# First layer: the experts' network moved from a stage of its own into the rounds of the attention

## The reference, cut to what matters

```python
xn = _layernorm(x)
# s: attention, 16 heads of 8 channels
attn = softmax(q @ k.T / sqrt(8)) * head_mask      # per head, 512 x 512 scores
s = (attn @ v) @ Wo.T + bo
# g: a shared network and eight experts of which two count per token
shared_out = swiglu(xn @ w_shared_in) @ w_shared_out
probs = softmax(xn @ w_gate + gate_bias);  top 2 of 8 kept, the rest set to 0
hid = swiglu(xn @ w1_shared)                       # the same for all experts
routed_out = sum_e probs_e * (hid @ w2[e])
x = x + s * silu(shared_out + routed_out)
```

## Time and profile before

| | us |
|---|---|
| three executions | 4061.76, 4041.41, 4063.99 (median 4061.76) |
| the profiled execution: own time | 4054.44 |
| the profiled execution: span | 4053.1 |
| busy in the span | PE 3121.8, DVE 2586.1, ACT 2027.6, POOL 1555.6 |
| mean granted clock of PE | 0.836 |

### The profile page before, as it was taken

How to read it: one execution, slowest core, us unless ns; L and a number is a source line. 1 busy time by engine, 2 the same in 40 slices (tenths; PEclk the granted TensorE clock), 3 DMA queues, 4 the chain that set the end, 5 groups by cost and what they waited for, 6 DMA issues and landing times.

```text
span 4053.1 us, 40791 instructions
## 1 busy us (share of the span) xinstructions
PE 3121.8 (77%) x14850; PEld 1366.2 (34%) x14850; DVE 2586.1 (64%) x2891; ACT 2027.6 (50%) x3628; POOL 1555.6 (38%) x938
## 2 busy tenths in 40 slices
PE   5777877975567777777875879766687888888886
PEld 2111212341222222222322643322144554555544
DVE  4676672438998788888877234487726655555553
ACT  1454453124456766666565221567444555555654
POOL 2211100113457666666757002244414444444432
PEclk6788897986678878877777879888698998999998
DMA  3111200011111121121111001000000000000000
GB/s 86 38 36 26 43 7 2 0 55 48 35 35 36 31 56 35 35 51 40 33 24 44 10 0 64 21 21 21 21 0 19 19 19 10 19 19 10 19 10 31
DMA packets 79733, 114.60 MB, mean 28 GB/s; under 512 B 16270, under 2 KB 49422, under 8 KB 78106
## 3 DMA queue, kind: packets, MB, share of 16 engines
q1 hardware_dynamic: 68268, 103.33, 10.5%
q0 software_dynamic: 11264, 8.66, 1.6%
HBM read 37.96 MB, written 17.33 MB: 14 GB/s over the span
## 4 chain that ended last, share of the span: by engine, by line
PE 50%; DVE 21%; ACT 16%; issue 6%; POOL 3%; DMA 2%; SPq 1%; POOLq 0%; DVEq 0%; ACTq 0%
DVE layer_mamba_state L1335 7%; DVE psum L1323 4%; PE psum L1107 3%; PE psum L774 3%; PE psum L2455 3%; PE psum L1184 3%; ACT layer_mamba_decay L1261 3%; PE psum L2486 3%; ACT layer_exps L787 2%; PE psum L238 2%; PE psum L2149 2%; PE psum L226 2%; PE psum L900 2%; PE psum L232 2%; PE psum L822 2%
## 5 line engine op out<-in xcount | busy, mean ns | idle before, releaser
L1364 POOL TENSOR_TENSOR layer_mamba_state<-layer_mamba_state,layer_mamba_c 128x1024 f32<-128x1024 f32 x320 | 780.4, 2448 | 597.1 <-DVE layer_mamba_state L1335 588.6
L1335 DVE TENSOR_TENSOR_SCAN layer_mamba_state<-layer_mamba_decay,psum 128x1024 f32<-128x1024 f32 x320 | 731.5, 2286 | 43.7 <-ACT layer_mamba_decay L1261 11.5
L1184 PE MATMUL psum<-layer_mamba_state,two_to_one 128*64 128x512 f32 x1280 | 443.7, 785 | 121.1 <-DVE layer_mamba_x L1352 77.0
L1261 ACT ACTIVATE layer_mamba_decay<-layer_mamba_delta_wide,layer_weights 128x511 f32<-128x511 f32 x640 | 415.6, 711 | 74.5 <-DMA layer_mamba_delta_wide<-layer_mamba_delta 38.2
L1323 DVE TENSOR_TENSOR psum<-psum,layer_mamba_u_wide 128x1024 f32<-128x1024 f32 x320 | 393.4, 1229 | 62.9 <-PE psum L1142 26.2
L714 DVE TENSOR_REDUCE layer_peak<-psum 128x2 f32<-128x1024 f32 x256 | 308.7, 1222 | 123.0 <-PE psum L685 118.4
L787 ACT ACTIVATE layer_exps<-psum 128x1024 f32<-128x1024 f32 x256 | 249.8, 1030 | 223.2 <-PE psum L754 223.2
L2852 POOL TENSOR_TENSOR layer_p<-layer_p,layer_stats 128x512 f32<-128x512 f32 x128 | 133.0, 1040 | 294.5 <-DVE layer_stats L2775 294.4
L2646 ACT ACTIVATE layer_p<-psum,layer_stats 128x128 f32<-128x128 f32 x512 | 181.2, 369 | 127.9 <-DVE layer_stats L2768 126.3
L1142 PE MATMUL psum<-layer_mamba_bc,layer_mamba_pick 96*64 96x512 bf16 x768 | 165.1, 457 | 91.2 <-DVE psum L1323 67.5
L2839 POOL TENSOR_TENSOR layer_qk<-layer_qk,layer_v_between 128x1024 f32<-128x1024 f32 x64 | 150.4, 2350 | 217.7 <-DVE layer_v_between L2739 215.9
(11 more groups left out here) (349 smaller groups left out, 6257.2 us busy)
## 6 DMA issues: line engine op xcount, KB each, us to landing
layer_mamba_delta_wide<-layer_mamba_delta SPq DMA_DIRECT2D x160, 128.0 KB, 2.3
layer_mamba_u_wide<-layer_mamba_work SPq DMA_DIRECT2D x160, 128.0 KB, 2.4
layer_v_between<-layer_v SPq DMA_DIRECT2D x16, 512.0 KB, 4.3
qk_dram<-layer_qk_parts SPq DMA_DIRECT2D x16, 384.0 KB, 2.6
layer_q_rows<-qk_dram SPq DMA_DIRECT2D x96, 64.0 KB
layer_k_rows<-qk_dram SPq DMA_DIRECT2D x96, 64.0 KB
layer_v_between<-layer_v SPq DMA_DIRECT2D x16, 384.0 KB, 5.6
layer_weights<-weights_dram SPq DMA_DIRECT2D x1, 4147.0 KB, 12.3
```

Source lines behind the costliest of these rows:

```text
L1184: e = pe.matmul(c.psum[j * HALF:(j + 1) * HALF, self.sum_banks[h], :], c.two_to_one[:, :], self.state[i % len(self.state)][:, j, :], start ...
L1261: e = act.activation(decay[:, j, 1:SEQ], self.delta_wide[h][:, j, 1:SEQ], ACT.Exp, scale=rates[:, rate:rate + 1])
L1335: dve.tensor_tensor_scan(state, decay, self.fill.rearrange("p j t -> p (j t)"), 0.0, ALU.mult, ALU.add).then_inc(self.scanned, 1)
L1364: pool.tensor_tensor(state, state, self.both(self.c_wide[turn % self.C_BUFFERS][:, :]), ALU.mult).then_inc(self.multiplied, 1)
```

## The change

`Ffn0` is no stage of its own any more. Its object is given to `Attention0`, whose `run` weaves the expert generators in with the others:

- **The choice of experts.** `Route` yields between its operations. Its first 8 steps are woven with project(0), after it in each round; the rest goes ahead of maxima(0) and project(1) in each round. The 64 logit records stand in its first step, so on PE they come behind the query product of sequence 0 and ahead of its key product. The transposes, eight rounds of four, all use bank 6.
- **The network.** `ffn(b)` is the last generator of iteration b, one sequence at a time, on bank 7 alone, and is silent for the first 7 rounds. On PE the four products of xn stand in rounds 7, 10, 12 and 15, the spreading of experts 0 to 3 in rounds 17 to 20, the shared output product and the experts' products in rounds 21 (three products) and 22 (two), experts 4 to 7 likewise in rounds 24 to 27, 28 and 29 (two each). ACT has SiLU in rounds 8 and 13, a Copy of the first half's total in round 22 and the gate's SiLU in round 30; DVE has the two swiglu products in rounds 10 and 15, the eight scalings in rounds 17 to 20 and 24 to 27, and the sum of the halves in round 29 or 30.
- **The update of x.** POOL multiplies and adds for sequence b-1 in round 7 of iteration b; for the last one after the last divide.
- Buffers are shared: the scaled inputs lie where the attention keeps its normed heads, and the choice works where it keeps its heads. The layer ends with one meeting of the engines less.

The arithmetic is the same but for the order of the sum over experts, now two halves of four. The other user of `Route`, in the third layer, plays its steps to the end at once, in the old order.

```diff
@@ Attention0.__init__ and run
-        weave(self.run(self.pe_project, self.pe_maxima, self.pe_attend, self.pe_divide))
-        weave(self.run(self.act_project, self.act_maxima, self.act_attend, self.act_divide))
-        weave(self.run(self.dve_project, self.dve_maxima, self.dve_attend, self.dve_divide))
-        weave(self.run(self.pool_project, self.pool_maxima, self.nothing, self.nothing))
+        weave(self.run(self.pe_project, self.pe_maxima, self.pe_attend, self.pe_divide, ffn.pe, self.nothing, route.pe()))
+        weave(self.run(self.act_project, self.act_maxima, self.act_attend, self.act_divide, ffn.act, self.nothing, route.act()))
+        weave(self.run(self.dve_project, self.dve_maxima, self.dve_attend, self.dve_divide, ffn.dve, self.nothing, route.dve()))
+        weave(self.run(self.pool_project, self.pool_maxima, self.nothing, self.nothing, self.nothing, ffn.pool, blank(0)))
...
-        weave(on(project, 0))
-        weave(on(maxima, 0), on(project, 1))
+        weave(on(project, 0), islice(route, self.CHOICE_BEFORE))
+        weave(route, on(maxima, 0), on(project, 1))
         for b in range(SEQS + 1):
-            weave(on(divide, b - 1), on(attend, b), on(maxima, b + 1), on(project, b + 2))
+            weave(on(divide, b - 1), on(attend, b), on(maxima, b + 1), on(project, b + 2), on(ffn, b), on(update, b - 1))
@@ Ffn0
+    BANK, BEHIND, PART = 7, 7, EXPERTS // 2
...
+    def pe(self, b):
+        c, pe, hold, w, rhs, bank = self.c, self.c.pe, self.c.pe_hold, self.w, self.xn[:, b, :], self.c.psum[:, self.BANK, :]
+        yield from blank(self.BEHIND)
+        hold.wait_ge(self.loaded, 16)
         for i, name in enumerate(("w_shared_in", "w1_shared")):
+            c.wait_bank(self.BANK)
+            pe.matmul(bank, w[name][:, 0:P], rhs, start=True, stop=True).then_inc(self.halves_made, 1)
+            c.bank_read[self.BANK] = self.silu_made, 2 * b + i + 1
             yield from blank(3)
+            c.wait_bank(self.BANK)
+            pe.matmul(bank, w[name][:, P:2 * P], rhs, start=True, stop=True).then_inc(self.halves_made, 1)
+            c.bank_read[self.BANK] = self.glu_made, 2 * b + i + 1
+            yield from blank(2)
+        for part in range(2):
+            experts = range(part * self.PART, (part + 1) * self.PART)
+            for n in experts:
                 hold.wait_ge(self.route.rows_made, b + 1)
+                c.wait_bank(self.BANK)
+                pe.matmul(bank, c.pick[0:3 * EXPERTS, n:n + 1].broadcast_to([3 * EXPERTS, P]),
+                          self.route.rows[:, b * SEQ:(b + 1) * SEQ], start=True, stop=True).then_inc(self.weight_spread, 1)
+                c.bank_read[self.BANK] = self.scaled_made, EXPERTS * b + n + 1
+                yield
+            c.wait_bank(self.BANK)
+            if part == 0:
+                hold.wait_ge(self.glu_made, 2 * b + 1)
+                pe.matmul(bank, w["w_shared_out"], self.glu[0][:, :], start=True, stop=False)
+            for n in experts:
+                hold.wait_ge(self.scaled_made, EXPERTS * b + n + 1)
+                m = pe.matmul(bank, w["w2"][:, n * P:(n + 1) * P], self.scaled[:, n % self.PART, :],
+                              start=part == 1 and n == experts[0], stop=n == experts[-1])
+                if n % 2:
+                    yield
+            m.then_inc(self.summed, 1)
+            c.bank_read[self.BANK] = (self.first_kept, self.gate_made)[part], b + 1
             yield
+    def act(self, b):
+        yield from blank(self.BEHIND)
         for i in range(2):
             yield
+            hold.wait_ge(self.halves_made, 4 * b + 2 * i + 1)
...
+            act.activation(self.silu[:, :], c.psum[:, self.BANK, :], SILU).then_inc(self.silu_made, 1)
+            yield from blank(4)
+        yield from blank(self.PART + 1)
+        hold.wait_ge(self.summed, 2 * b + 1)
+        hold.wait_ge(self.glu_made, 2 * b + 2)
+        act.activation(self.silu[:, :], c.psum[:, self.BANK, :], ACT.Copy).then_inc(self.first_kept, 1)
+        yield from blank(self.PART + 4)
+        hold.wait_ge(self.added, b + 1)
+        hold.wait_ge(self.x_made, b - 1)
+        act.activation(self.gated[b % 2][:, :], c.psum[:, self.BANK, :], SILU).then_inc(self.gate_made, 1)
+        yield
+    def dve(self, b):
...
+            dve.tensor_tensor(self.glu[i][:, :], self.silu[:, :], bank, ALU.mult).then_inc(self.glu_made, 1)
...
+        for part in range(2):
+            hold.wait_ge(self.summed, 2 * b + part)
+            for n in range(part * self.PART, (part + 1) * self.PART):
+                hold.wait_ge(self.weight_spread, EXPERTS * b + n + 1)
+                dve.tensor_tensor(self.scaled[:, n % self.PART, :], self.glu[1][:, :], bank, ALU.mult).then_inc(
+                    self.scaled_made, 1)
+                yield
+            yield from blank((3, 1)[part])
+        hold.wait_ge(self.summed, 2 * (b + 1))
+        hold.wait_ge(self.first_kept, b + 1)
+        dve.tensor_tensor(bank, bank, self.silu[:, :], ALU.add).then_inc(self.added, 1)
+        yield
@@ layer0
-            Attention0(c, ctx, xn, w, loaded, attn)
-            c.end_stage()
-        with ExitStack() as ctx:
-            Ffn0(c, ctx, x, xn, attn, wf, ffn_loaded)
+            Attention0(c, ctx, xn, w, loaded, attn, Ffn0(c, ctx, x, xn, attn, wf, ffn_loaded))
             c.end_stage()
```

More of the change, by code:

```diff
@@ L1 @@
 from contextlib import ExitStack
+from itertools import islice
 import concourse.bass as bass
@@ L370, in pe @@
         m.then_inc(self.logits_made, 1)
+        yield from blank(self.CHOICE_STEPS)
         hold.wait_ge(self.step, self.weighed)
@@ L382, in pe @@
         for b in range(SEQS):
-            hold.wait_ge(self.rows_made, b - 1)
+            hold.wait_ge(self.rows_made, b + 1 - len(set(self.banks)))
             for k in range(BLOCKS):
@@ L387, in pe @@
             m.then_inc(self.parts_turned, 1)
-        for at in range(2):
-            c.bank_read[6 + at] = self.rows_made, SEQS - 1 + at
+            yield
+        for b in (SEQS - 2, SEQS - 1):
+            c.bank_read[self.banks[b % 2]] = self.rows_made, b + 1
     def act(self):
         c, act, hold = self.c, self.c.act, self.c.act_hold
+        yield from blank(2)
         hold.wait_ge(self.step, 3)
         act.activation(self.prob[:, :, :], self.prob[:, :, :], ACT.Exp).then_inc(self.exp_made, 1)
+        yield from blank(self.CHOICE_STEPS - 2)
         if self.whole_rows:
@@ L827, in pe_divide @@
         for g in range(QUADS0):
-            m = pe.matmul(bank, w["wo_rows"][:, g * P:(g + 1) * P], self.normed[g][:, :], start=g == 0,
+            m = pe.matmul(bank, w["wo_rows"][:, g * P:(g + 1) * P], self.normed[g], start=g == 0,
                           stop=g == QUADS0 - 1)
@@ L856 @@
 class Ffn0:
+    BANK, BEHIND, PART = 7, 7, EXPERTS // 2
     def __init__(self, c, ctx, x, xn, attn, w, loaded):
-        self.c, self.xn, self.w, self.loaded = c, xn, w, loaded
-        self.route = Route(c, ctx, xn, w["w_gate"], w["gate_bias_rows"], loaded, False, False)
-        buf = lambda name, s=[P, SEQ]: [c.buffer(ctx, f"{name}{i}", s) for i in range(2)]
-        self.silu, self.scaled = buf("silu"), buf("scaled", [P, 2, SEQ])
-        self.glu = [buf("shared"), buf("hidden")]
-        self.update = Update(c, ctx, x, attn)
@@ new lines, in __init__ @@
+        self.c, self.x, self.xn, self.attn, self.w, self.loaded = c, x, xn, attn, w, loaded
+        self.heads, self.scaled = (c.buffer(ctx, name, [P, QUADS0, SEQ]) for name in ("heads", "scaled"))
+        self.route = Route(c, ctx, xn, w["w_gate"], w["gate_bias_rows"], loaded, False, False, (6, 6),
+                           self.heads.rearrange("p g t -> p (g t)"))
+        self.silu = c.buffer(ctx, "silu", [P, SEQ])
+        self.glu = [c.buffer(ctx, name, [P, SEQ]) for name in ("shared", "hidden")]
@@ new lines, in __init__ @@
+        self.gated = [c.buffer(ctx, f"gated{s}", [P, SEQ]) for s in range(2)]
+        signal = lambda name: c.sem(ctx, name)
+        self.halves_made, self.silu_made, self.glu_made = (signal(n) for n in ("halves_made", "silu_made", "glu_made"))
+        self.weight_spread, self.scaled_made, self.summed = (signal(n) for n in ("weight_spread", "scaled_made", "summed"))
+        self.first_kept, self.added = signal("first_kept"), signal("first_added")
+        self.gate_made, self.gate_used, self.x_made = (signal(n) for n in ("gate_made", "gate_used", "x_made"))
@@ L938, in pool @@
-    def pool(self, b, s):
-        yield from blank(6 + EXPERTS + 1)
-        self.update.pool(b, s, b // 2)
+            hold.wait_ge(self.halves_made, 4 * b + 2 * i + 1)
+            hold.wait_ge(self.glu_made, 2 * b + i)
+            hold.wait_ge(self.added, b)
+            act.activation(self.silu[:, :], c.psum[:, self.BANK, :], SILU).then_inc(self.silu_made, 1)
[3 more added lines that the diff above has]
+        hold.wait_ge(self.glu_made, 2 * b + 2)
@@ L941, in pool @@
+    def pool(self, b):
```

(7 more changed lines are left out.)

124 lines of the change are left out of this document (45 added, 79 removed).

## The result

The changed kernel takes 4172.91 us (median; 4169.28 to 4174.22) against 4054.49 (4041.41 to 4063.99) of the kernel before, run beside it: the ratio is 1.0293 [1.0258, 1.0328], 118 us slower. The forecast was 4095 in 4005 to 4150, so it had the sign and missed the size, and the time lies above the range.

A forecast was written before the change was run, and what follows sets the result against it. The prediction took a 2.83 us turn, a closed loop through PE and ACT, to bound the attention's even part. -149.6 + 146 + 16 + 4 + 20 = +36 on 4054.4 gave 4090.8, stated as 4095, range 4005 to 4150.

The forecast's parts named there:

- the two stalls: SiLU among the exponentials, rounds 8 and 13: each blocks ACT 3.2 us and costs 2.5, so 5.0 us per sequence.
- the gate: SiLU in round 30, ahead of exponential 31 and serial work: its 3.2 us count in full less 0.1, so 3.1.
- stage removed: From the attention's last output to the next layer's first product: 149.6 of 152.6 us go.
- products, bursts, scalings: Per sequence on PE and DVE: products of xn 2.1 us, nine products in bursts 6.4, eight spreadings and scalings 4.3.
- last sequence: Last sequence, without maxima: ACT is the bound, so SiLU count in full; 16 us (10 to 20).
- prologue: Choice of experts moved there: logits ahead of the key product delay keys and loads, +4 us (0 to 10).
- PE's clock: Stalls in rounds 8 and 13 may drop PE to half clock: half of 14 at 2.8 us, +20.
- by its weighing alone: In the attention's turn: at half clock it loses over 1.3 us by the weighing alone.
- Rival C: Clock falls after each stall, rounds 8 to 16 and bursts meet half clock: 11 us per sequence, 4147; chance 0.20.
- B: Network overlaps as meant in the attention's even part, DVE bounding it: 3985 us; chance 0.17.
- D: Table loads around the SiLU don't come, or pairs in hand absorb ACT's delay: 4005 us; chance 0.10.
- E: Each table switch on ACT costs the skill page's price, 1.3 us more: +54 on the forecast, 4149; chance 0.03.

The follow-up runs named there:

- e1: The changed kernel with exponentials in place of all three SiLU per sequence, so no table changes and other gate values: 4037.95 us, 0.9974 of the kernel before.
- e5: The kernel before plus an unread SiLU of xn on ACT behind exponentials 8, 13 and 30 of every sequence: 4164.92 us, 1.029.
- e2: The changed kernel plus two unread PE products in each of the three SiLU pauses of seven iterations: 4122.24 us, 1.0176 of the kernel before.
- e6: The kernel before plus an unread exponential of xn on ACT behind exponentials 8, 13 and 30 of every sequence: 4057.37 us, 1.0011.
- e12: The kernel before plus three unread SiLU per sequence, together behind ACT's negation of the maxima, where ACT waits anyway: 4047.31 us, 0.9988.
- e10: e9 plus one unread PE product in each of rounds 1 to 4 of seven iterations: 4011.64 us, 0.9915 of the kernel before.
- e11: e1 without the eight spreadings and scalings per sequence, so routing weights are left out: 3987.72 us, 0.9843 of the kernel before.
- e9: e7 with the choice begun three rounds later, so the logits stand behind the key product: 4014.6 us, 0.9903 of the kernel before.
- e4: The changed kernel with SiLU computed from tanh, three more DVE operations per sequence: 4049.54 us, 0.9998 of the kernel before.
- e7: The kernel before with only the choice moved, plus six unread PE products where PE waits for the maxima: 4018.63 us, 0.9925.

## Why the prediction was right or wrong

The account of the first layer, forecast against measured (intervals between the negations of maxima, then the rest up to the next norm). Of the forecast 146 for seven iterations, 53.2 are counted for the SiLU: 5.0 for the two stalls and 2.6 for the gate, whose other 0.5 an exponential in its place would cost as well:

| step | forecast | measured |
|---|---|---|
| stage removed | -149.6 | -149.6 |
| seven iterations: products, bursts, scalings | 92.8 | 110.2 (e1) |
| seven iterations: SiLU and clock | 53.2 + 20 | 126.1 (after less e1) |
| last sequence | 16 | 28.0 (15.0 in e1) |
| prologue | 4 | 7.1 |
| sum | +36 | +121.8 |

**The failed step is "PE's clock", 20 us: half of 14 stalls at 2.8 each.** In its place stand some 73 us, if the SiLU's serial 53.2 are right (126.1 - 53.2). Three things in it were wrong. Nearly all stalls bring the clock down (20 of 21), not half. There are three per iteration, not two: the gate's pause of 2.86 us was costed in full as serial time, and its effect on the clock was never asked for. And I took the length of the low stretch from one row with its 7 us; here stretches of up to 20.5 us follow. Seven stalls of 7 us are 49 us at half clock; the clock's records have 358 us of it in these iterations and 164 in e1, so 194. At the 1.3 us that a turn of 4.13 loses (e5) they are 61, an estimate that accounts for most of the 73. What sets a stretch's length isn't shown: e5 has 3.4 and 13.7 us with the same turns behind. e5 (+113 without experts), e1 (-135), e2 (-51 with the loads kept) show the step from three sides; e6 excludes the place, and e12 that a load costs by itself wherever it stands.

The price of a turn at half clock was right, but not its reading "by its weighing alone": the weighing takes 1.93 for 1.07, 0.87 more, and the rest of the 1.3 is in the scores of the turn. The 2.8 us for a stretch of 7 weren't worked out; at 1.3 per 4.13 it would be 2.2, at e10's price 3.3.

**The SiLU stalls as such** were right: 3.2 us of ACT, and pauses of 2.54 and 3.39 against the replayed 2.6, the second 0.8 longer. M(10) does go late by about the replayed amount; only what it meets is another clock.

**Rival C had the mechanism** (the clock falls after each stall, and the bursts meet it) and was given 0.20. Its 11 us per iteration for the clock, 4147, was still too small, as it too left out the gate's stall. Its mark in the trace, iterations of over 105 us with low clock, is what came. Its places were not quite these: the low stretch behind the first stall doesn't reach the second (0.95 in the row of 475.00), and the long one stands behind round 13, in the scaling rounds. What I held against it, the bursts behind, come too late: PE is busy 17.91 of 19 us in the row of 482.00 at 0.50, ahead of all but the first products of the burst.

**The rest of the sum.** The products, bursts and scalings are 110 us for 93, 2.5 per iteration more. Of these some 1.0 is the scalings' (5.3 for 4.3, e11); the other 1.5 lie in the products and bursts or in the three 0.6 us of ACT that e1 keeps, and which of them wasn't told apart. The last sequence without stalls takes 15.0 for some 8, and that stays open. The prologue takes 7.1 for 4. Of it 0.7 is the stage's later start (31.82 for 31.11); the logits need 12.44 us ahead of the key product where they took 10.21. The order of logits and key product is worth 3.7 (e9), so the forecast's 4 was right for what it counted; 2.8 us stay with the logits behind the key product (81.5 for 78.7 from the first product to the negation), and no run tells their cause.

```profile
32.79 12.44 PE L371 MATMUL psum<-layer_weights,xn 128*128 128x8 f32 x64
45.08 2.05 PE L632 MATMUL psum<-xn,layer_weights 128*128 128x512 f32 x2
```

**The other rivals.** B (overlap, 3985) didn't come even without stalls: e4 is at 4049.5, and the iteration 18 us over 74. D (no loads) is refuted by 48 of them. E, the price of the Trainium skill's page "ScalarE: Activation LUTs" (section "What ACT_TABLE_LOAD costs") with a drain beside the load, is refuted by the row: 464.40 + 1.28 = 465.68 and the SiLU starts at 465.70; 466.31 + 1.28 = 467.59 and the exponential starts at 467.61. The time came out above E's 4149 without any drain. The Trainium skill's rule to batch by table set (the same page, section "Table sets: the hidden batching unit") is borne out by e1 and e4, though e12 shows its limit: in idle time the change of table is free.

## What to carry to other kernels

A stall on one engine is to be priced by what it does to PE's clock as well: first the pause, then the turns behind it at half clock. One row gives the price of a turn (1.3 us here) but not the length of the stretch, which was 3.4 to 20.5 us in one and the same iteration: take the longest and the shortest as the ends of the range, and count every stall, also one that stands ahead of a wait. Before a function goes between others on ACT, look for a form in the same table (here tanh for SiLU, 123 us), or for a place where ACT waits anyway (nothing, for 113 us elsewhere). Work moved beside other work needs holes of its own size in the fixed order: the network cost 15.7 us per sequence inside, without any table change (e1, 110.2 / 7), for 15.5 outside. That the products' length of 0.9 against holes of 0.84 is why was argued, and no run tried it.

## What the runs showed of the hardware that was not expected

- In the changed kernel, pauses of PE of 2.54 to 3.39 us are followed by stretches of 3.4 to 20.5 us at half clock; in the longest PE is busy for 94% of the time by the records (17.91 of 19 us).
- The stretch's length doesn't follow from the turns behind it: 3.4 us behind the pause of 2.57, 13.7 behind that of 3.04, with the same turns (e5).
- Work that nobody reads makes the program faster: two products in each of three pauses per iteration gain 51 us (e2), six in one pause gain 14 (e7).
- Iterations with the same instructions take 69.3 or 74.1 us, by whether one low stretch of 10.2 us occurs (e10).
